# A transformer block with 16 experts on one core: the experts' results scattered to token order inside the expert loop, in place of gathers after it

## What is computed

```python
x = x + attention(layernorm(x), W_Q, W_K, W_V, W_O)
n = layernorm(x)
shared = (silu(n @ shared_w_gate.T) * (n @ shared_w_up.T)) @ shared_w_down.T
shared = shared * sigmoid(n @ shared_gate_w.T)
probs = softmax(n @ gate_w.T)            # over 16 experts
rw, sel = top_k(probs, 2); rw = rw / rw.sum(-1)
g, h = split(einsum('nd,edf->nef', n, w_gate_up))
expert_out = einsum('nef,efd,ne->nd', silu(g) * h, w_down, combine)   # combine holds rw at sel
x = x + expert_out + shared
```

## Time and profile before

| what | value |
|---|---|
| median of 3 runs | 771.03 us (770.41 to 773.2) |
| profiled execution, span from the first to the last instruction | 768.6 us |
| what lies around the span | not given for this execution; the runs' median is 2.43 us above the span |
| mean granted TensorE clock | 0.966 |
| PE busy | 698.2 us (91%) |
| DVE busy | 523.6 us (68%) |
| ACT busy | 400.9 us (52%) |
| POOL busy | 330.9 us (43%) |
| moved by DMA | 164.02 MB, 213 GB/s on average |

### The profile page before, as it was taken

One profiled execution on the slowest core, in us unless ns is written; L12 is line 12 of the kernel. 1 busy time (PEld: TensorE's weight loads), 2 busy tenths in 40 slices (PEclk: granted clock), 3 DMA queues, 4 the chain that ended last, 5 costly groups with the idle time before them and its releaser, 6 DMA issues. The chain is left out here.

```text
span 768.6 us, 16584 instructions
## 1 busy us (share of the span) xinstructions
PE 698.2 (91%) x5906; PEld 555.8 (72%) x5906; DVE 523.6 (68%) x1158; ACT 400.9 (52%) x779; POOL 330.9 (43%) x678
## 2 busy tenths in 40 slices
PE   3589999999999999999999687999899999899992
PEld 3456576676767667676656586888699999798882
DVE  4387788887888888787853678456655555438874
ACT  3126667566675757757666415334556666512330
POOL 5205445273552725525283327777300000067774
PEclk9789999999999999999999979999899999999997
DMA  4958577576875758847433297656446556378764
GB/s 131 320 202 305 195 273 244 208 247 243 302 262 188 257 205 302 276 169 241 153 112 108 85 387 239 213 188 209 158 139 190 187 186 193 112 231 266 255 222 134
DMA packets 100398, 164.02 MB, mean 213 GB/s; under 512 B 7648, under 2 KB 74208, under 8 KB 96096
## 3 DMA queue, kind: packets, MB, share of 16 engines
q1 hardware_dynamic: 94176, 146.18, 56.3%
q0 software_dynamic: 6144, 16.79, 6.6%
HBM read 86.66 MB, written 76.02 MB: 212 GB/s over the span
## 5 line engine op out<-in xcount | busy, mean ns | idle before, releaser
L685 DVE TENSOR_REDUCE neg_max<-ps_w 128x1 f32<-128x512 f32 (+3 forms) x352 | 202.7, 633 | 43.7 <-PE ps_w L790 43.5
L604 ACT ACTIVATE probs<-ps_w 128x512 f32<-128x512 f32 x320 | 165.3, 617 | 10.1 <-PE ps_w L806 10.0
L435 POOL TENSOR_TENSOR pool_scratch<-minus_half 1x1 f32<-1x1 f32 x190 | 34.8, 183 | 232.2 <-ACT probs L604 199.4
L1202 POOL DMA_INDIRECT ex<-yg_dram,slots x64 | 64.9, 1014 | 150.2 <-DMA yg_dram<-y 131.0
L467 POOL TENSOR_SCALAR_AFFINE_SELECT probs<-probs 128x256 f32<-128x256 f32 (+1 forms) x224 | 93.8, 430 | 0.0
L1190 POOL DMA_INDIRECT xg_dram<-srow,slots x64 | 70.7, 1104 | 32.7 <-issue 19.2
L1233 ACT ACTIVATE rows_held<-ps_f 128x512 f32<-128x512 f32 (+1 forms) x42 | 25.0, 596 | 110.4 <-PE ps_f L190 110.4
L817 PE MATMUL ps_w<-probs,v_aug 128*32 128x512 f32 (+3 forms) x1024 | 77.2, 443 | 0.3 <-DVE logits_all L713 0.3
L188 PE MATMUL ps_f<-stacks 128*128 128x512 f32 x154 | 61.6, 400 | 4.1 <-DVE rows_held L1433 4.1
L817 PEld LDWEIGHTS ps_w<-probs,v_aug 128*32 128x32 f32 x1024 | 31.2, 111 | 41.1 <-issue 32.7
L190 PE MATMUL ps_f<-stacks 128*128 128x512 f32 x154 | 60.5, 393 | 0.0
(11 more groups left out here) (187 smaller groups left out, 1768.0 us busy)
## 6 DMA issues: line engine op xcount, KB each, us to landing
qk_dram<-projected SPq DMA_DIRECT2D x96, 256.0 KB, 6.2
stacks<-qk_dram SPq DMA_DIRECT2D x16, 1024.0 KB, 7.4
heads_held<-qk_dram SPq DMA_DIRECT2D x12, 1024.0 KB, 6.4
xg_dram<-zeros SPq DMA_DIRECT2D x20, 512.0 KB, 10.6
srow<-xg_dram SPq DMA_DIRECT2D x40, 256.0 KB, 2.9
ex<-experts SPq DMA_DIRECT2D x4, 1536.0 KB, 14.8
yg_dram<-projected SPq DMA_DIRECT2D x20, 256.0 KB, 2.2
yg_dram<-y SPq DMA_DIRECT2D x20, 256.0 KB, 2.2
```

The costliest lines, as they stand in the source:

```text
L435: ticks = Ticks(pool, pool_ticks, lambda: pool.tensor_tensor(out=pool_scratch[:, 0:1], in0=minus_half[0:1, 0:1], in1=minus_half[0:1, 0:1], ...
L604: act.activation(probs[:, g, p * PAIR + half * BANK:p * PAIR + (half + 1) * BANK], ps_w[:, plan.bank(kind, which, half), :], ACT.Exp).then ...
L685: dve.tensor_reduce(out=neg_max[u][:, qt, first:first + len(heads)], in_=bank[:, 0:len(heads) * width].rearrange("p (h n) -> p h n", h=len ...
L1202: pool.indirect_dma_start(out=back[:, m, c, :], out_offset=None, in_=yg_rows, in_offset=bass.IndirectOffsetOnAxis(ap=slots[:, c, m:m + 1], ...
```

## The change

Each row carries its place along. `xg_dram` rows get two more numbers (ROW = 258): the place of the token's first result in token order, and the token's first expert. POOL and DVE write these tags into memory of `top`, once; SP puts them beside the rows ahead of the scatter, by a load of 2 x 4 numbers a partition per batch. The zeros that fill the padding carry a place beyond the end.

In the expert loop DVE compares, for each of a pair's two tiles, the carried expert with the tile's own and adds the outcome to the carried place (`places`). POOL then scatters the pair's rows from `y_e` to token order in `yt_dram`, two indirect DMAs a pair, with a bounds test that drops the padding's rows. SP no longer stores pairs. POOL's 64 gathers are gone; SP loads each batch's results with one plain load of 1 MiB (8 KiB a partition), all eight at the start of the third stage, and the first two of y1 and x1 of batch 4 among them.

```diff
+TAGS = 2
+ROW = D + TAGS
+FRESH = 2 * B * S
...
-            sp.dma_start(srow[:, b % 2], xn2_v[b]).then_inc(rows_in[b % 2], 16)
+            sp.dma_start(srow[:, b % 2, :, 0:D], xn2_v[b]).then_inc(rows_in[b % 2], 16)
+
+        def tags_of(b):
+            if b == 0:
+                sp.wait_ge(tags_made, 2)
+            sp.dma_start(srow[:, b % 2, :, D:ROW], tags[:, b * TB:(b + 1) * TB, :]).then_inc(rows_in[b % 2], 16)
...
         def load_pair(q):
             if q >= FOUR:
                 sp.wait_ge(m_xT, q - (FOUR - 1))
+                sp.wait_ge(placed, q - (FOUR - 1))
...
+        def load_back(b):
+            sp.dma_start(back[:, b * TB:(b + 1) * TB].rearrange("p t c d -> p (t c d)"), yt_v[b]).then_inc(back_in[b], 16)
...
         def second_half(b, more):
-            load_x1(b)
             if b == FIRST:
+                load_back(0)
                 load_y1(0)
+                load_x1(b)
+                load_back(1)
                 load_y1(1)
+                for old in range(2, B):
+                    load_back(old)
             else:
+                load_x1(b)
                 load_y1(b - 1)
             load_next_xn(b)
...
+        pool.wait_ge(args_ready, 1)
+        pool.iota(tags[:, :, 0], pattern=[[2 * P * TB, B], [2, TB]], base=0, channel_multiplier=2 * TB, allow_small_or_imprecise_dtypes=True).then_inc(tags_made, 1)
...
-        for m in range(NT):
-            if m >= TB:
-                pool.wait_ge(gathered[m % TB], 32 * (m // TB))
-            for c in range(2):
-                pool.indirect_dma_start(out=back[:, m, c, :], out_offset=None, in_=yg_rows,
-                                        in_offset=bass.IndirectOffsetOnAxis(ap=slots[:, c, m:m + 1], axis=0)).then_inc(gathered[m % TB], 16)
+        for q in range(TILE_PAIRS):
+            pool.wait_ge(placed, q + 1)
+            pool.wait_ge(m_y, q + 1)
+            for t in range(2):
+                pool.indirect_dma_start(out=yt_dram, out_offset=bass.IndirectOffsetOnAxis(ap=places_of_rows[:, 2 * q + t:2 * q + t + 1], axis=0),
+                                        in_=y_e[q % FOUR][:, t, :], in_offset=None, bounds_check=FRESH - 1, oob_is_err=False).then_inc(moe_out[q % FOUR], 16)
...
+        def places(q):
+            dve.wait_ge(moe_in[q % FOUR], 16 * (q // FOUR + 1))
+            for t in range(2):
+                tile = 2 * q + t
+                made = dve.scalar_tensor_tensor(out=places_of_rows[:, tile:tile + 1], in0=xg[:, q % FOUR, t, D + 1:ROW], scalar=expert_f[:, tile:tile + 1],
+                                                in1=xg[:, q % FOUR, t, D:D + 1], op0=ALU.not_equal, op1=ALU.add)
+            made.then_inc(placed, 1)
+
         def lower_x(q):
+            places(q)
             dve.wait_ge(m_xT_hi, q + 1)
```

More of the change, by code:

```diff
@@ L517, in _ @@
             chain.step(pool.memset(v_aug[n][:, :, :, DH:STRIP], 1.0))
-        pool.memset(zeros[:, :], 0.0).then_inc(zeros_made, 1)
+        pool.memset(zeros[:, 0:D], 0.0).then_inc(zeros_made, 1)
+        pool.iota(zeros[:, D:ROW], pattern=[[-FRESH, TAGS]], base=FRESH, channel_multiplier=2, allow_small_or_imprecise_dtypes=True).then_inc(zeros_made, 1)
         def shared_lower(n):
@@ L1034, in build_ffn @@
     m_down, m_y = sem("m_down"), sem("m_y")
-    gathered = [sem(f"gathered{n}") for n in range(TB)]
+    back_in, tags_made, tagged, placed = [sem(f"back_in{b}") for b in range(B)], sem("tags_made"), sem("tagged"), sem("placed")
     consts_done, consts_raw, args_ready, exps_ready = sem("consts_done"), sem("consts_raw"), sem("args_ready"), sem("exps_ready")
@@ L1045, in build_ffn @@
     out_v = out.rearrange("b (t p) d -> b p t d", p=P)
-    xg_pairs, yg_pairs = (v.rearrange("(q t) p d -> q p t d", t=2) for v in (xg_dram, yg_dram))
+    xg_pairs = xg_dram.rearrange("(q t) p d -> q p t d", t=2)
+    yt_v = yt_dram[0:FRESH].rearrange("(b p r) d -> b p (r d)", b=B, p=P)
     SCATTERS = 2 * TB * 16
@@ L1103, in first_half @@
                 rows_of(ahead)
+                tags_of(ahead)
             sp.wait_ge(y_done, TB * (b + 1))
@@ L1162, in _ @@
             rows_of(b)
+        for b in range(2):
+            tags_of(b)
         for n in range(LOADS):
@@ L1371, in experts_of_tiles @@
             for n in range(1, 4):
-                do(dve.scalar_tensor_tensor(out=four[:, :, 0], in0=four[:, :, n], scalar=float(E ** n), in1=four[:, :, 0], op0=ALU.mult, op1=ALU.add))
-            dve.tensor_copy(experts_of_four[:, 0:TILE_PAIRS:2], four[:, :, 0]).then_inc(routed, 1)
+                do(dve.scalar_tensor_tensor(out=packed[:, :], in0=four[:, :, n], scalar=float(E ** n), in1=packed[:, :] if n > 1 else four[:, :, 0],
+                                            op0=ALU.mult, op1=ALU.add))
+            dve.tensor_copy(experts_of_four[:, 0:TILE_PAIRS:2], packed[:, :]).then_inc(routed, 1)
         def split_xT(b, ks=range(DK)):
@@ L1451, in add_first @@
         def add_first(m):
[L1452 removed]
+            if m % TB == 0:
+                dve.wait_ge(back_in[m // TB], 16)
             add_rows(0, m, first_added)
@@ L1653, in block_program @@
     qk_dram = dram("qk_dram", [UNITS, 2, P, SLOTS_U, S])
-    xg_dram, yg_dram = (dram(n, [MOE_TILES, P, D]) for n in ("xg_dram", "yg_dram"))
+    xg_dram, yt_dram = dram("xg_dram", [MOE_TILES, P, ROW]), dram("yt_dram", [FRESH + 2 * P, D])
     with ExitStack() as whole:
@@ L1668, in block_program @@
         with ExitStack() as ctx:
-            build_ffn(nc, ctx, stacks, projected, w_lo, x_lower, rows_held, heads_held, logits_all, top, index, slots, experts_of_four, weight, gate, x1_dram, xn2_dram, x2T_dram, xg_dram, yg_dram, y1_dram,
+            build_ffn(nc, ctx, stacks, projected, w_lo, x_lower, rows_held, heads_held, logits_all, top, index, slots, experts_of_four, weight, gate, x1_dram, xn2_dram, x2T_dram, xg_dram, yt_dram, y1_dram,
                       ident, experts, out)
```

38 lines of the change are left out of this document (17 added, 21 removed).

## The result

The changed kernel takes 775.78 us (median of 8 runs, 774.53 to 778.28) against 772.71 for the kernel before in the same comparison (8 runs); the ratio is 1.0042, with a 95% interval of 1.0023 to 1.0061. So it is 3.1 us slower; the forecast was 2.5 us more than the median then known, and the time lies 2.3 us above the forecast, inside the range. The difference is real, but it is smaller than the 0.5% that the prediction asked for: by the ratio this is its "same" (0.38) and not the likelier "slower" (0.47), although 775.78 lies above the bound of 774.9 that it had worked out from the median then known.

What follows compares the result with a forecast made beforehand. PE was taken to bound the expert loop and shared expert, with a tail of gathers behind it. 768.6 - 7.9 + 0.2 + 0.6 + 7.5 + 2.1 = 771.1, with 2.43 above the span 773.5 us; range 764 to 785.

Steps and rivals of the forecast that it cites:

- same: Whole kernel: a time between the bounds 767.2 and 774.9 us, within the 0.5% a measurement can tell; chance 0.38.
- slower: Whole kernel: a time above the bound of 774.9 us; chance 0.47.
- Step 1: Tail behind PE: the gathers leave it and DVE adds the last tiles without that wait; gain 7.9 us.
- Step 2: Expert loop, POOL: scatters of 0.96 us, two with gaps 2.52 against a pair's 2.80, 0.28 left; no cost.
- Step 3: Expert loop, DVE: two small operations a pair, taken as 0.2 us, show only ahead of the first pair; +0.2 us.
- Rival C: Expert loop: POOL's scatters block DVE's two-input operations, 1.2 us a pair beyond the cover, so 821 us; chance 0.05.
- Step 4: Start of build_ffn: tag loads of 1,024 small packets stand ahead of the experts' weights and x1; +0.6 us, kept 0 to 4.7.
- The small packets' upper bound of 4.7: Start of build_ffn: 1,024 tag packets of 8 bytes, if each costs as much as an average one, 4.7 us.
- Step 5: Third stage: eight loads in SP's queue hold batch 4's store to 704.7, delaying batch 6's input; PE stands still 7.5 us.
- Step 6: Third stage, behind PE's stall: PE runs at a lowered clock for some microseconds; +2.1 us, 1.6 to 2.6.
- 2.43 added at the end: Whole kernel: the median of three runs, 771.03 us, lies 2.43 above the profiled span of 768.6; added to the sum.
- Rival A: Third stage: the gain stays, as batch 4's store or batch 6's input isn't held up; 763.9 us; chance 0.16.

Runs made afterwards that it cites:

- e4_pool_load: The changed kernel with one more POOL operation, a waited-for memset of 512 elements a partition, ahead of every pair's two scatters: 808.44 us, ratio 1.0485.
- e1_spread: The changed kernel with only SP's third-stage order changed: x1 of batch 4 first, three 1 MiB loads at the start, the others two at a time later: 767.53 us, 0.9973.
- e7: The same kernel as e1_spread, run again for a closer interval: 768.93 us, ratio 0.9961.
- e3_pool_queue: The changed kernel with the eight 1 MiB loads issued by POOL into its own queue and x1 of batch 4 first on SP: 775.28 us, ratio 1.0059.
- e2_input_first: The changed kernel with the load of batch 6's transposed input issued ahead of the eight 1 MiB loads: 776.01 us, ratio 1.0064.
- e10_y1_early: e5 plus 4 KB pieces of x1 and y1, DVE's small operations behind its subtraction, and y1 of batches 2 and 3 right behind batch 6's input: 766.56 us, 0.9922.
- e11_one_by_one: e10_y1_early with each of the last five 1 MiB loads issued alone, right behind the store of a finished batch: 762.68 us, ratio 0.9881.
- e5: e1_spread with x1 of batch 0 loaded ahead of the last two of the experts' four loads: 766.04 us, ratio 0.9929.

## Why the prediction was right, step by step

**Step 1, the tail, right.** Forecast: the end 6.35 us behind PE's end and 7.9 us gained; measured 6.10 and 8.15.

**Step 2, POOL, right.** Forecast a scatter of 0.96 and 0.28 us of room; measured 0.98 to 0.99 and 0.22. The bounds test and the dropped rows add no more than the 0.02 to 0.03 between them, if the two scatters are alike otherwise. Beyond that room the slope is the one forecast (e4_pool_load).

**Step 3, DVE, right in place, low in size.** The two small operations take 0.35 us together ahead of the first pair and hold its subtraction back by 0.38, where 0.2 was taken. In the loop their cover held: PE is busy from 565 to 665 without a break. Rival C is out: the subtraction beside the scatters takes 0.69 us, as in the earlier trace rows.

**Step 4, the start of `build_ffn`, right.** x1 landed 11.3 us after its issue (469.74 - 458.41), 1.05 later than in the earlier trace rows; to PE's restart it cost 1.00. One execution is not enough for such a size: in the six profiles with this start (the change, e1 to e4 and e7) DVE goes on 10.55 to 12.25 us after the issue, mean 11.3, and PE restarts 30.0 to 31.7 us after its first matmul of `build_ffn`, mean 30.8, where before it took 30.2; so 0.6, as forecast. In the table's profile the way from the restart to the first pair adds 0.61 (the 0.38 of step 3 in it), and the loop gives 0.69 back: PE ran at a mean clock of 0.76 from 558 to 565, where it had 0.56 from 553 to 560 before. Together the piece is 0.92 longer; 0.8 had been taken for steps 3 and 4. The small packets' upper bound of 4.7 was far off.

**Step 5, the queue, right in mechanism and size, its reason too narrow.** Forecast a pause of 7.5 us, SP held to 704.7; measured 8.10 and 710.19, or 706.0 when the third stage's later start (4.17) is taken off. On the way two errors cancelled: POOL had fallen behind by the end of the loop and its last scatter came at 678.30, 1.0 later than forecast after the same shift, but the first load was issued 2.2 us behind it, not 3.5. From the first load's issue to SP's next transfer behind the store it took 29.70 us, 1.6 more than forecast. e1_spread shows that the loads in front are the cause. But the step argued from the place in one queue. e3_pool_queue shows that another queue would not have helped: both queues moved equally many packets, and the one with the small ones got 0.49 MB beside 3.61. And e2_input_first shows that the transposed input was not the only late transfer, as the step had it: with it on time, a late y1 cost 7.01 us.

**Step 6, the clock, mechanism right, size low.** Forecast 2.1 us behind the pause, measured 2.9: six microseconds at 0.50. Not forecast: a further 0.9 us at the third stage's start, where PE ran at 0.50 from 676 to 680, after 0.88 us idle as before. The mean clock of the stage's first four microseconds was 0.57 in both profiles without the change; with it, it was 0.50 in three, 0.58 to 0.62 in six and 1.00 in two (e10 and e11). So the 0.9 is not shown to be the change's, and why this differs no run shows.

**The sum, closer than its terms.** The forecast's terms add up to 2.5 us and the medians differ by 3.1. In the two profiles the same terms add up to 4.65 (-8.15, 0.92, 8.10, 2.88 and 0.90 at the third stage's start), with the queue and the clock 2.3 above their forecast. The profiles lie 4.8 further apart than the medians, so how much of the 2.3 is the change's stays open, and that the sum fits better than its terms is in part luck. Of the 2.43 added at the end, 1.7 to 1.8 lie around a span; the rest is a difference between executions.

**What the sum didn't hold** is the 3.25 us ahead of PE's first matmul of `build_ffn`. The seven profiles of kernels that share the change's first block word for word (the change, e1 to e5 and e7) have that matmul at 444.19 to 449.51, mean 446.5; the two that share the block of before at 444.19 and 445.74, mean 445.0. So some 1.7 of the 3.25 are differences between executions. Whether the other 1.6 or so belong to the wider rows, which the first block fills with zeros, stays open, as the seven alone spread over 5.3 us; it was not tried by itself.

Rival A did not happen, but e11_one_by_one shows that a time like it was to be had: its median of 762.68 lies below the 763.9 forecast for it. The steps that changed SP's order, the earlier x1 among them, are those with a gain (0.9961, 0.9929, 0.9881); what the 4 KB pieces and DVE's other order add was not told apart from nothing.

## What to carry to other kernels

When work leaves the end of a kernel, look for what the new transfers stand in front of: a bulk load that nothing needs yet goes behind the small transfers that the next stage waits for, one piece at a time. Moving it to another engine's queue is no remedy by itself: here the two queues shared the DMA engines by number of packets, so that the one with 1 KB pieces got 0.49 MB beside 3.61 in 8 KB pieces; with 4 KB pieces it got 1.40 beside 2.78. After an engine's wait is mended, read the trace again: here the transfer next in the queue was nearly as late each time (e2_input_first, e10_y1_early).

## What was not expected of the hardware

- Two queues with work moved 492 and 497 packets in 10 us, 3.61 MB and 0.49 MB: equal numbers, unequal bytes. A store of 512 KB in 1 KB pieces held SP for 22.87 us beside them, in 4 KB pieces for 8.82.
- POOL's scatter begins 0.78 us after the end of an operation that it waits for, though only 0.30 lie between two scatters without a wait. In the changed kernel POOL is busy 1.96 of a pair's 2.80 us, but of the 0.84 left only 0.22 are room.
- The load of x1 behind 1,024 packets of 8 bytes landed only 1.05 us later than without them; in six profiles it was 0.3 to 2.0, mean 1.0.
